# One change to a state-space and mixture-of-experts kernel: the step size in two halves around the routing, a new end, and another place for the expert pairs

## The reference, cut to what matters

```python
xn = layernorm(x)                       # input of both parts
# state space
xn2 = layernorm(xn) * norm_w + norm_b
delta, B, C = split(xn2 @ x_proj_w.T)   # 128, 64, 64 columns
dt = softplus(delta @ dt_proj_w.T + dt_proj_b)
h[t] = exp(dt * A) * h[t-1] + dt * B * xn2      # per channel and state
y[t] = sum_n h[t] * C_used              # C of t % 64
ssm = (y + xn * D_param) @ out_proj_w.T
# experts
scores = sigmoid(xn @ gate_w.T)         # choice with bias, groups of 8, top 4 groups, top 6
routed = sum_e w_e * relu2(xn @ w1[e]) @ w2[e]
shared = relu2(xn @ w_up) @ w_down
out = x + ssm + shared + routed
```

## Time and profile before

| | us |
|---|---|
| median of 3 runs | 1054.94 (1049.82 to 1057.08) |
| the profiled execution, its own time | 1047.24 |
| its span, first to last instruction | 1045.5 |
| VectorE busy | 923.7 (88%) |
| TensorE busy | 726.6 (70%) |
| GpSimd busy | 578.1 (55%) |
| ScalarE busy | 544.6 (52%) |

### The profile page before, as it was taken

The page is one execution under the profiler, slowest core; times in us unless marked ns, Lnnn a source line. Parts: engine busy times, 40 slices in busy tenths (PEclk is TensorE's granted clock), DMA queues, the critical chain, the costliest instruction groups (busy, mean ns, idle before and its releaser), DMA issues. The chain is left out here.

```text
span 1045.5 us, 18790 instructions
## 1 busy us (share of the span) xinstructions
PE 726.6 (70%) x6663; PEld 454.5 (43%) x6664; DVE 923.7 (88%) x842; ACT 544.6 (52%) x807; POOL 578.1 (55%) x391
## 2 busy tenths in 40 slices
PE   1868683014556988989988999988999875333336
PEld 1835352001222655656655666665665542111125
DVE  6579976889999999999999999999999999999963
ACT  0204054543334777877878777877787853221200
POOL 5001147777503656667676666757676675777710
PEclk9679897555555899999999999999998975555557
DMA  9990004693222999999999999999999963433332
GB/s 333 354 342 23 0 26 165 226 307 116 89 53 69 263 277 286 287 286 286 291 290 292 275 264 288 283 262 285 299 286 277 268 189 99 108 101 98 99 110 80
DMA packets 178653, 217.83 MB, mean 208 GB/s; under 512 B 50433, under 2 KB 137858, under 8 KB 178306
## 3 DMA queue, kind: packets, MB, share of 16 engines
q1 hardware_dynamic: 169346, 191.45, 64.9%
q0 software_dynamic: 9216, 25.18, 7.7%
HBM read 144.61 MB, written 71.83 MB: 207 GB/s over the span
## 5 line engine op out<-in xcount | busy, mean ns | idle before, releaser
L962 DVE TENSOR_TENSOR_SCAN H<-ps,U 128x1024 f32<-128x1024 f32 x256 | 581.2, 2283 | 25.6 <-ACT ps L687 21.7
L687 ACT ACTIVATE ps<-ps,Acur 128x1024 f32<-128x1024 f32 x256 | 278.9, 1090 | 242.0 <-PE ps L1126 240.5
L591 POOL TENSOR_TENSOR U<-X,B 128x1024 f32<-128x1024 f32 x100 | 237.5, 2375 | 198.4 <-DVE H L962 141.7
L1126 PE MATMUL ps<-PK,sel 24*128 24x512 bf16 x824 | 162.3, 447 | 222.4 <-DVE H L962 145.2
L1115 PE MATMUL ps<-H,CB 128*32 128x128 f32 x4096 | 240.9, 395 | 5.7 <-DVE H L962 5.7
L1126 PEld LDWEIGHTS ps<-PK,sel 24*128 24x128 bf16 x824 | 45.2, 93 | 332.1 <-issue 292.2
L1115 PEld LDWEIGHTS ps<-H,CB 128*32 128x32 f32 x4096 | 143.2, 130 | 85.8 <-issue 26.5
L591 POOL TENSOR_TENSOR U<-GS,B 128x1024 f32<-128x1024 f32 x50 | 120.0, 2401 | 28.5 <-DVE H L962 24.6
L621 POOL DMA_INDIRECT WE<-yg_d,slot x96 | 93.8, 977 | 41.5 <-issue 22.4
L577 POOL DMA_INDIRECT xg_d<-XN,slot x96 | 98.7, 1028 | 30.0 <-issue 28.8
L1210 PE MATMUL ps<-WE,AS 128*128 128x256 f32 x320 | 95.4, 423 | 0.0
(11 more groups left out here) (146 smaller groups left out, 615.9 us busy)
## 6 DMA issues: line engine op xcount, KB each, us to landing
X<-g_d SPq DMA_DIRECT2D x200, 256.0 KB, 6.3
WE<-w_exp_dram SPq DMA_DIRECT2D x160, 256.0 KB, 5.0
xg_d<-CB SPq DMA_DIRECT2D x20, 1024.0 KB, 11.2
XG<-xg_d SPq DMA_DIRECT2D x80, 256.0 KB, 6.6
yg_d<-YO SPq DMA_DIRECT2D x80, 256.0 KB, 6.3
PK<-pk_d SPq DMA_DIRECT2D x64, 128.0 KB, 6.3
pk_d<-GS SPq DMA_DIRECT2D x16, 256.0 KB, 3.8
X<-x_dram SPq DMA_DIRECT2D x4, 512.0 KB, 5.6
```

The source lines that it names most:

```text
L591: nc.gpsimd.tensor_tensor(U[:, c % 4, :], rows, B2[:, b * L:(b + 1) * L], ALU.mult).then_inc(u_pool, 1)
L687: nc.scalar.activation(a_tile(c), a_tile(c), ACT.Exp, scale=Acur[:, b, pair:pair + 1]).then_inc(a_ready, 1)
L962: V.tensor_tensor_scan(H[:, (s // GRP % 2) * GRP + s % GRP, :], a_tile(s), U[:, s % 4, :], 0.0, ALU.mult, ALU.add).then_inc(scan_done, 1)
L1126: return mm(ps[:, bank, :], sel[32 * g:32 * g + ROWS, c % SUB, :], PK[32 * g:32 * g + ROWS, c // SUB % NPK, :], start=True, stop=True)
```

## The change

- **Norms.** Statistics start with the first quarter of x; the second norm's factor is worked out from the first norm's variance (one Sqrt for both), and ScalarE writes XN2 tile by tile.
- **dt in two halves.** `steps_of_two(0)` (first half of the channels, both batch entries) runs ahead of the routing, `steps_of_two(1)` behind it. Two q go through the stages together, each with its own buffers. Everything of the kind g (product, rest, third part) moves from VectorE to GpSimd (`g_split`).
- **Routing.** GpSimd multiplies OH by the scores (`weight`, 6) and by the positions for three k (`position`); VectorE sums. ScalarE evacuates B and the prefix sums.
- **SP.** 7 of 20 zeroing DMAs go out first, 13 after the stores of the first half of the parts.
- **GpSimd.** 11 scatters lie among the second half's `g_split`, the other 85 around the shared expert's sums; all 96 stand ahead of GpSimd's first product of a scan (DEFER = 0).
- **Shared expert.** It takes `(D_param*out_proj)` along as two more matmuls per down step (dwo); its last 6 steps move into the first 12 scans of block 0.
- **Pairs.** PAIR_SLOT starts with the third even step of block 1 (FIRST = 2), and each eighth is left out (REST = 8).
- **End.** y comes back in five loads, most of it during the last block, into X; ScalarE brings it into token order in xnT (`turn`); TensorE multiplies tile by tile over 7 banks; VectorE adds in XN, from which the output is stored.

The diff, cut to its core:

```diff
-REST = 7
+REST = 8
+FIRST = 2
+DEFER = 0
 NMT = 2 * NPAIR
-NXT = NMT + 4
+NXT = NMT
...
-        PAIR_SLOT = [n for n in range(SLOTS - 2) if n % REST != REST - 1][:NPAIR]
+        PAIR_SLOT = [n for n in range(FIRST, SLOTS - 2) if (n - FIRST) % REST != REST - 1][:NPAIR]
...
-        JOBS = ([("xnT", q, "act") for q in range(8)] + [("logit", q, "act") for q in range(2)]
-                + [("xn2T", q, "dve") for q in range(8)] + [("B", q, "dve") for q in range(4)]
-                + [("dpre", q, "act") for q in range(4)] + [("C", q, "dve") for q in range(2)]
-                + [("prefix", q, "dve") for q in range(4)] + [("dt", q, "dve") for q in range(8)])
+        JOBS = ([(kind, 2 * g + h, who) for g in range(4) for kind, who in (("xn2T", "dve"), ("xnT", "act")) for h in range(2)]
+                + [("dpre", q, "act") for q in range(3)] + [("dt", q, "dve") for q in range(2)]
+                + [("dpre", 3, "act")] + [("dt", q, "dve") for q in range(2, 4)]
+                + [("logit", q, "act") for q in range(2)] + [("B", q, "act") for q in range(4)]
+                + [("C", q, "dve") for q in range(2)]
+                + [("prefix", q, "act") for q in range(4)] + [("dt", q, "dve") for q in range(4, 8)])
...
+        SH_FIRST, SH_LAST = 12, 26
+        def shared_bank(step):
+            return 4 + step % 2 if step < SH_LAST else 6
...
+            store_zeros(0, 7)
...
+            for q in range(2):
+                store_parts(q, 0, split_t)
+            for q in range(2):
+                store_parts(q, 1, split_g)
+            sp.wait_ge(parts_stored, 16 * 12)
+            sp.wait_ge(zeros_stored, 16 * 11)
+            for n in range(NPK - 1):
+                load_sub(0, n)
+            store_zeros(7, NXT // 8)
+            sp.wait_ge(aneg_ready, 2)
+            load_rates(0, 0)
...
+                    if it == PRE and s == 2 * FIRST - 4:
+                        sp.wait_ge(scattered, 16 * TT * TOPK)
+                        for p in range(MBUF):
+                            load_inputs(p)
+                            load_weights(experts_of(p), p)
...
+                    if it == BLK - 1 and s == 2 * GRP - 1:
+                        sp.wait_ge(u_pool, by_gpsimd(BLK, 0) + 2)
+                        for par in range(2):
+                            sp.wait_ge(s_ys[par], 32 * ((BLK - 1) * 2))
+                        sp.dma_start(yT[:, 0, :, :], ys_d[0:P, :, :]).then_inc(s_y[0], 16)
+                        sp.dma_start(yT[0:P - CH, 1, :, :], ys_d[P:D - CH, :, :]).then_inc(s_y[1], 16)
...
+            sp.wait_ge(s_ys[0], 32 * (BLK * 2))
+            sp.dma_start(yT[P - CH:P - CH // 2, 1, 1, :], ys_d[D - CH:D - CH // 2, 1, :]).then_inc(s_y[3], 16)
             store_group(BLK * 4 - 1, BLK - 1, SL - GRP)
-            for par in range(2):
...
+            def g_split(q, stage):
+                h, b = q // 2, q % 2
+                if stage == 0:
+                    pool.wait_ge(dt_done, q + 1)
+                    nc.gpsimd.tensor_tensor(l_t[b], z_t[b], xn2T[:, h, b * L:(b + 1) * L], ALU.mult).then_inc(g_done, 1)
+                elif stage == 1:
+                    pool.wait_ge(first_g, q + 1)
+                    nc.gpsimd.tensor_tensor(u_t[b], l_t[b], prt3[b][:, 2, :], ALU.subtract).then_inc(rest_g, 1)
+                else:
+                    pool.wait_ge(second_g, q + 1)
+                    nc.gpsimd.tensor_tensor(prt[b][:, 1, :], u_t[b], prt3[b][:, 3, :], ALU.subtract).then_inc(split_g, 1)
...
+            def weight(k):
+                pool.wait_ge(oh_ready, k + 1)
+                if k >= 2:
+                    pool.wait_ge(wn_summed, k - 1)
+                nc.gpsimd.tensor_tensor(weighted[k % 2], OH[k], sc, ALU.mult).then_inc(oh_sc, 1)
+            def position(k):
+                pool.wait_ge(pos_ready, 1)
+                pool.wait_ge(wn_summed, TOPK)
+                nc.gpsimd.tensor_tensor(weighted[k // 2], OH[k], pos, ALU.mult).then_inc(oh_pos, 1)
...
+            for stage in range(3):
+                for q in range(2):
+                    g_split(q, stage)
+            add_shared(0, 4)
+            for k in range(TOPK):
+                weight(k)
+            for k in range(0, TOPK, 2):
+                position(k)
+            add_shared(4, 8)
             pool.wait_ge(slots_ready, 1)
-            pool.wait_ge(zeros_stored, 16 * ((NXT + 7) // 8 + 4))
-            for k in range(TOPK):
-                for t in range(TT):
-                    scatter(k, t)
-                if k == 0:
-                    add_shared(TT - 4, TT)
+            pool.wait_ge(zeros_stored, 16 * (NXT // 8 + 4))
+            for n in range(8):
+                scatter(n)
+            for stage in range(3):
+                for q in range(2, 4):
+                    g_split(q, stage)
+                scatter(8 + stage)
+            add_shared(8, 12)
+            for n in range(11, 44):
+                scatter(n)
+            add_shared(12, TT)
+            for n in range(44, TT * TOPK - DEFER):
+                scatter(n)
...
+            nc.scalar.activation(rstd[:, :, :], rtmp[:, :, :], ACT.Sqrt).then_inc(sqrt_ready, 1)
+            for t in range(TT):
+                act.wait_ge(xn_ready, t + 1)
+                nc.scalar.activation(XN2[:, t, :], XN[:, t, :], ACT.Copy, scale=rstd[:, 1, t:t + 1]).then_inc(xn2_ready, 1)
...
+            exp_of(0)
+            exp_of(1)
+            log_of_one_plus(0)
+            log_of_one_plus(1)
+            first_part(0, 0)
+            first_part(1, 0)
+            first_part(0, 1)
+            second_part(0, 0)
+            first_part(1, 1)
+            second_part(1, 0)
+            second_part(0, 1)
+            second_part(1, 1)
...
+            def turn(h, b, first, last):
+                yv = yT[:, h, b, :].rearrange("p (r c) -> p c r", r=PERIOD)[:, first:last, :]
+                zv = xnT[:, h, b * L:(b + 1) * L].rearrange("p (c r) -> p c r", r=PERIOD)[:, first:last, :]
+                nc.scalar.copy(zv, yv).then_inc(y_turned, 1)
...
+            def steps_of_two(h):
+                two = (2 * h, 2 * h + 1)
+                for q in two:
+                    b = q % 2
+                    if q >= 2:
+                        dve.wait_ge(rest_g, q - 1)
+                        dve.wait_ge(first_t, q - 1)
+                    for c in range(2):
+                        n = JN["dt", 2 * q + c]
+                        dve.wait_ge(job_done, n + 1)
+                        V.tensor_scalar(z_t[b][:, 512 * c:512 * c + 512], ps[:, job_bank(n), :], vec[:, h, 2:3], None, ALU.add)\
+                            .then_inc(dve_evac, 1)
+                    dve.wait_ge(dve_evac, evac_no(n))
+                    V.scalar_tensor_tensor(e_t[b], z_t[b], -1.0, z_t[b], ALU.mult, ALU.min).then_inc(z_ready, 1)
+                for q in two:
+                    b = q % 2
+                    dve.wait_ge(exp_ready, q + 1)
+                    if q >= 2:
+                        dve.wait_ge(split_g, q - 1)
+                    link(V.tensor_scalar(u_t[b], e_t[b], 1.0, None, ALU.add))
+                    link(V.scalar_tensor_tensor(u_t[b], u_t[b], -1.0, e_t[b], ALU.add, ALU.subtract))
+                for q in two:
+                    b = q % 2
+                    dve.wait_ge(ln_ready, q + 1)
+                    link(V.tensor_tensor(l_t[b], l_t[b], u_t[b], ALU.subtract))
+                    V.scalar_tensor_tensor(z_t[b], z_t[b], 0.0, l_t[b], ALU.max, ALU.add).then_inc(dt_done, 1)
+                    dve.wait_ge(dt_done, q + 1)
+                for q in two:
+                    b = q % 2
+                    dve.wait_ge(first_t, q + 1)
+                    V.tensor_tensor(e_t[b], z_t[b], prt3[b][:, 0, :], ALU.subtract).then_inc(rest_t, 1)
+                    dve.wait_ge(rest_t, q + 1)
+                for q in two:
+                    b = q % 2
+                    dve.wait_ge(second_t, q + 1)
+                    if q >= 2:
+                        dve.wait_ge(parts_stored, 16 * 12)
+                    V.tensor_tensor(prt[b][:, 0, :], e_t[b], prt3[b][:, 1, :], ALU.subtract).then_inc(split_t, 1)
...
+            steps_of_two(0)
+            dve.wait_ge(act_evac, evac_no(JN["logit", 1]))
+            dve.wait_ge(bias_in, 16)
+            dve.wait_ge(consts, 6)
+            dve.wait_ge(split_t, 2)
+            dve.wait_ge(g_done, 2)
...
-                dve.wait_ge(oh_ready, k + 1)
-                link(V.tensor_tensor(ra, OH[k], sc, ALU.mult))
-                link(V.tensor_reduce(wn[:, :, k], t64(ra), AX.X, ALU.add))
...
+            for k in range(TOPK):
+                dve.wait_ge(oh_sc, k + 1)
+                V.tensor_reduce(wn[:, :, k], t64(weighted[k % 2]), AX.X, ALU.add).then_inc(wn_summed, 1)
+            dve.wait_ge(wn_summed, TOPK)
...
+            steps_of_two(1)
+            dve.wait_ge(split_t, 4)
+            dve.wait_ge(g_done, 4)
...
+                    pe.wait_ge(dwo_ready, 2)
+                    for h in range(2):
```

(48 more changed lines are left out.)

448 lines of the change are left out of this document (226 added, 222 removed).

## The result

The changed kernel takes 1004.18 us (median of 4 runs, 1002.18 to 1004.54); before took 1055.06 (4 runs, 1049.82 to 1057.08). The ratio is 0.9521, interval 0.9485 to 0.9558. The forecast was 1004. The total hits; its terms do so less well, and two errors cancel. The profiled execution of after took 1004.18 us, with a span of 1002.4.

The account below looks back on a forecast made before the run. VectorE's scans were taken to set the pace, unchanged from scan 33 on. 33 us won ahead of scan 33 and 17.7 at the end, given as 50.5, off the median 1054.9 gave 1004; own range 990 to 1017.

Parts of the forecast that it names:

- Part 1: Start to routing: with GpSimd and VectorE taking turns, logits at 67.1, routing at about 69, some 19 us later than before.
- Rival one: Ahead of the slots: GpSimd and VectorE share nothing, routing starts at 62.4, gain 70, time 985; chance 12%.
- Part 2: Routing: about 82 us instead of 99.6, slots at 150; GpSimd's share of the weights brings no gain.
- Rival two: Routing: GpSimd's products with a bf16 tile are slow, 4.7 us each, 19 more on the path, 1023; chance 13%.
- The late zeroing: SP's 13 late zeroing DMAs, 2.85 us each, run from about 79 to 119 and stay hidden.
- Part 3: Slots to first scan: only half the dt work left, first scan 38 us after the slots, where 78.8 stood.
- Part 4: Scatters up to scan 33: last done 150.1 us after the slots, a stall of 4; scan 33 at 303, 33 won.
- Part 5: Expert pairs among the scans: equal work in new places, between -2 and +4 us, taken 0.
- Rival three: Blocks 1 to 6 and seven scans after: denser pairs bind TensorE; from 0.26 us more a scan no gain; chance 2%.
- Part 6: Behind the last scan: the end takes 24.3 us against 42.0, 17.7 won.
- rival four: Prologue: GpSimd's start to scan lags by 40 us or more, scan 33 stays, about 1050; chance 3%.
- failure signs: Wrong if slots before 140 or behind 160, GpSimd waits over 10 us for a scan, or 32 scans exceed 87 us.

Follow-up runs that it names:

- the deferring run: The changed kernel with six of the 96 scatters put behind GpSimd's first product (DEFER = 6): 1007.71 us in its one run.
- before again: The kernel before, run once more without any edit for its trace alone: 1057.17 us.
- the kernels of the same work: The changed kernel once more without edit, 998.25 us, and the changed kernel with xg_d four tiles larger (NXT = NMT + 4), 1000.83 us.

## Why the prediction was right

By its own steps, with after's profiled execution:

- **Part 1** forecast logits at 67.1 and the routing at about 69. ScalarE's Exp was done at 64.8, and the routing's first operation started at 64.87. Rival one (sharing nothing) had 62.4, and fell with the stretched rows above. The taking of turns was right. Of the 2.3 us at the logits, 1.4 stood already at the first dt (47.2 instead of 48.6), ahead of any turn, so the turns were priced at most about 0.9 too high. The step "its first operation waiting for GpSimd's last split" is half right: no semaphore holds VectorE there and it starts 1.6 before that split ends, but its operation then reads 2.18 instead of 0.68 and ends behind it. The second operation starts at 67.1, where the forecast makes it 69.7.
- **Part 2** forecast about 82 us for the routing (150 less 69 is 81) and "no gain" from GpSimd's share: it took 82.4 from 64.87, 1.5 of them in that first operation. The 24.2 us for the weights measured 22.1 (97.4 to 119.5), where 22.6 stood before, and the run with them on VectorE confirms the zero. Rival two (bf16 products slow) fell: four of them in a row took 8.44, 2.11 each, less than the fp32 product's 2.34. (The late zeroing was to end at 119 by a sum that comes to 116; it ended at 107.5. Hidden either way.)
- **Part 3** forecast the first scan at S+38: it came at S+36.5.
- **Part 4** forecast the last scatter done at S+150.1 and a stall of 4: S+147.9 and 3.2, and the deferring run shows the cause. The 2.2 us stand already behind the eleventh scatter (done at S+34.7 instead of 36.8); from there the spacing of 1.265 holds. By the printed 0.96 no stall would stand there. What becomes of the additions when GpSimd has less to do before them, a wait in hiding, the forecast had not looked for.
- **Part 5**, steady blocks and pairs "between -2 and +4, taken 0": the profiles of after and before differ by 13.2 here, and the step that failed is an unspoken one, that one profiled execution stands for the blocks. Two profiles of before give 516.5 and 526.3. The zero itself fits the second: from scan 33 to the last scan's end before again took 677.9, after 681.0 and 675.7. Rival three (denser pairs bind TensorE, from 0.26 us more a scan) fell: before with the new pattern took 1.0014 (0.9976 to 1.0052) of before's time.
- **Part 6** forecast -17.7: measured -18.1, and -17.3 against before again.

The sum: scan 33 is 38.0 earlier rather than 33, the tail gives 18.1, together 56 where 50.5 was forecast, 5.6 more; that also ends rival four (the gain eaten in the prologue). The blocks took 13.0 back, so the spans differ by 43.1 and the profiled execution stands at 1004.18, not at the forecast's 996.7. The median was met because the forecast had added the 7.7 us by which before's median stood above its profiled execution: that covered 7.7 of the 13.0, and the 5.3 that are left cancel against the 5.6. This last cancelling is luck. On the chip of the later runs the kernels of the same work stood at 998.25 and 1000.83 against 1055.68, a gain of 55 to 57, about the 56 of the landmarks. So the prologue was undersized by 5 us (slots 2.7 early, nearly all of it standing at the routing's second operation; 1.5 in the dt part and 0.9 at the scatters), which is half a per cent and inside the range.

Of the failure signs, slots and GpSimd's wait did not show; "a block of 32 scans over 87 us" did (87.5, 87.3, 90.2 ...), and shows in before again as well (90.8, 89.8), so it was no good sign: its bound was set from one execution.

## What to carry to other kernels

Work handed to GpSimd beside two-input VectorE work was no help here. Price it as 3.1 to 3.4 us of GpSimd for an operation of 1024 columns, with 1.8 to 2.0 lost by each VectorE operation that it holds up, and compare with VectorE's 1.2 for the same; then ask who waits for GpSimd's result. Beside scans that read PSUM, and beside reductions, neither was lengthened in these rows; there it may pay, which no run here priced. When an engine is freed, look at the next thing that it waits for in its queue, as the shared additions and SP's wait for the last scatter here. And before a difference of 1% in a DMA-heavy stretch is explained, profile the old kernel twice.
